# A banded attention step: the mask leaves the score product and becomes a multiplication of the exponentials on GpSimd

## The reference

```python
x = iter_norm_whiten(x, gamma, beta)             # whitening with a 64x64 matrix from the covariance
t = tokens(x)                                    # 16 x 3136 x 64
n = layernorm(t)                                 # queries, keys and values alike
windows = pad(n, 16)[:, arange(N)[:, None] + arange(33)[None, :]]
scores = einsum("bnd,bnwd->bnw", n, windows) * 64 ** -0.5
out = einsum("bnw,bnwd->bnd", softmax(scores), windows)
t = t + (layernorm(out) * gamma1 + beta1)
t = t + moe(layernorm(t))                        # 8 experts, the best 2 of each token, gelu
```

## Time and profile before

| what | value |
|---|---|
| median of the 3 runs | 1188.25 us (1186.55 to 1189.57) |
| the profiled execution: its own time, its span | 1198.36 us, 1196.5 us |
| mean granted clock of PE, of its full 2.4 GHz | 0.942 |
| PE busy | 1115.0 us, 93% |
| DVE busy | 913.3 us, 76% |
| ACT busy | 614.6 us, 51% |
| POOL busy | 146.7 us, 12% |

### The profile page before, as it was taken

How to read it: one execution, slowest core, us unless ns; L and a number is a source line. 1 busy time by engine, 2 the same in 40 slices (tenths; PEclk the granted TensorE clock), 3 DMA queues, 4 the chain that set the end, 5 groups by cost and what they waited for, 6 DMA issues and landing times.

```text
span 1196.5 us, 29077 instructions
## 1 busy us (share of the span) xinstructions
PE 1115.0 (93%) x9550; PEld 748.8 (63%) x9550; DVE 913.3 (76%) x2575; ACT 614.6 (51%) x975; POOL 146.7 (12%) x173
## 2 busy tenths in 40 slices
PE   7958999989899898989869999999999999999998
PEld 6836777777777777777655455555555555555553
DVE  6943678877777787878768877777787777777775
ACT  0015566656556565656435555555555555555553
POOL 6021222222222222222210000000000000000000
PEclk9957999999989898989759999999999999999999
DMA  9501121211211111211111222222222222222222
GB/s 291 195 22 27 48 60 50 61 48 46 61 44 51 47 54 47 54 47 35 37 54 39 69 69 68 68 68 69 69 69 69 69 68 68 68 69 69 69 69 47
DMA packets 136171, 78.69 MB, mean 66 GB/s; under 512 B 112416, under 2 KB 134176, under 8 KB 135344
## 3 DMA queue, kind: packets, MB, share of 16 engines
q1 hardware_dynamic: 127040, 64.78, 20.9%
q10 hardware_dynamic: 8064, 12.85, 2.9%
q0 software_dynamic: 1008, 0.43, 0.2%
HBM read 52.33 MB, written 25.69 MB: 65 GB/s over the span
## 4 chain that ended last, share of the span: by engine, by line
PE 64%; DVE 22%; ACT 5%; issue 5%; SPq 2%; DMA 1%; DVEq 0%; POOL 0%; ACTq 0%; POOLq 0%
PE p L1119 16%; PE p L1094 15%; PE p L1104 9%; DVE t_s L786 5%; PE p L1029 5%; PE p L1063 4%; PE p L934 3%; PE p L1041 3%; DVE sm L737 2%; PE p L927 2%; ACT prob L517 2%; DVE st L747 2%; PE p L1115 2%; DVE xn_s L780 2%; PE p L1058 2%
## 5 line engine op out<-in xcount | busy, mean ns | idle before, releaser
L546 ACT ACTIVATE arena<-p,b_s 128x896 f32<-128x896 f32 x224 | 225.4, 1007 | 245.9 <-PE p L1094 245.2
L843 DVE TENSOR_TENSOR arena<-arena,p 128x896 f32<-128x896 f32 x224 | 242.9, 1084 | 93.0 <-PE p L1104 89.8
L1119 PE MATMUL p<-arena,w_s 128*64 128x448 f32 x896 | 215.7, 560 | 0.3 <-DVE arena L843 0.3
L1094 PE MATMUL p<-thl,w_hi 128*128 128x448 f32 x448 | 165.0, 450 | 0.5 <-DVE thl L817 0.5
L1104 PE MATMUL p<-arena,selector 128*128 128x448 bf16 x448 | 124.7, 360 | 3.5 <-DVE arena L843 3.0
L1094 PE MATMUL p<-thl,w_lo 128*128 128x448 f32 x448 | 127.6, 366 | 0.0
L1104 PEld LDWEIGHTS p<-arena,selector 128*128 128x128 bf16 x448 | 25.5, 97 | 161.6 <-issue 116.1
L737 DVE TENSOR_REDUCE sm<-sq 128x14 f32<-128x896 f32 (+1 forms) x59 | 61.3, 1039 | 81.3 <-ACT sq L487 59.3
L1094 PEld LDWEIGHTS p<-thl,w_hi 128*128 128x128 f32 x448 | 85.8, 192 | 21.4 <-issue 1.0
L418 POOL TENSOR_TENSOR yb<-yb,bet 128x448 f32<-128x448 f32 x56 | 59.2, 1058 | 317.4 <-DVE xn_s L780 317.4
L1094 PEld LDWEIGHTS p<-thl,w_lo 128*128 128x128 f32 x448 | 84.9, 190 | 7.3
(11 more groups left out here) (174 smaller groups left out, 1817.5 us busy)
## 6 DMA issues: line engine op xcount, KB each, us to landing
tn_spill<-tnt_s ACTq DMA_DIRECT2D x56, 224.0 KB, 2.0
arena<-tn_spill SPq DMA_DIRECT2D x56, 224.0 KB, 3.4
t_s<-tn_spill SPq DMA_DIRECT2D x56, 224.0 KB, 2.5
arena<-in_x_dram SPq DMA_DIRECT2D x112, 96.0 KB, 2.1
out_dram<-arena SPq DMA_DIRECT2D x112, 96.0 KB, 1.8
resid<-in_x_dram SPq DMA_DIRECT2D x6, 1568.0 KB, 13.2
resid<-in_x_dram SPq DMA_DIRECT2D x6, 384.0 KB, 7.1
arena<-in_x_dram SPq DMA_DIRECT2D x112, 16.0 KB, 2.0
```

What stands on the lines that cost most here:

```text
L546: a.activation(hid[:, j % 2, :].rearrange("p (h n) -> p h n", h=H), (p34 if j % 2 == 0 else p56)[:, :, 0:CH], ACT.Gelu, bias=b1_s[:, j:j + ...
L843: v.tensor_tensor(gated[:, j % 2, :].rearrange("p (h n) -> p h n", h=H), hid[:, j % 2, :].rearrange("p (h n) -> p h n", h=H), p01[:, :, 0: ...
L1094: last = t.matmul(bank[:, h, 0:CH], w[:, 128 * j:128 * (j + 1)], thl[:, c, h, :], start=(k == 0), stop=(k == 1))
L1119: last = t.matmul(p2[64 * h:64 * h + 64, 0:CH], w2_s[:, j, :], gated[:, j % 2, h * CH:(h + 1) * CH], start=False, stop=(j == 3))
```

## The change

The mask product on PE goes, and with it the tile `outside`. Scores are no longer added to something; every one of their products starts its own sum. In its place POOL multiplies the exponentials, in place, by `band`, a 96x64 tile of ones and zeros that is laid over all 14 blocks of the chunk. This multiplication stands in POOL's step behind its two additions. PV waits for it (`s_pm`) and no longer for the exponentials.

```diff
@@ gpsimd, preparation @@
             v.tensor_copy(eye_h[:, :], eye[:, :])
-            v.tensor_scalar(outside[:, :].rearrange("p (n q) -> p n q", q=BLK),
-                            band[:, :].unsqueeze(1).to_broadcast([KEYS, 4 * H, BLK]), -1.0, OUTSIDE, ALU.add, ALU.mult)
@@ gpsimd, step(g, c, has) @@
                     v.tensor_tensor(resid[:, bass.ds(q * CH, CH)].rearrange("p (b c) -> p b c", b=NB), t_s[:, sl],
                                     yb[:, cq, :, 0:C], ALU.add).then_inc(s_t2, 1)
+                if has(2):
+                    q = g - 2
+                    wait(pool, s_p, q + 1)
+                    if has(3):
+                        wait(pool, s_t2, q)
+                    if has(1):
+                        wait(pool, s_yb, q + 2)
+                    scores = prob[:, :, :].rearrange("p h (b n) -> p (h b) n", b=NB)
+                    v.tensor_tensor(scores, scores, band[:, :].unsqueeze(1).to_broadcast([KEYS, H * NB, BLK]),
+                                    ALU.mult).then_inc(s_pm, 1)
@@ tensor, step(g, c, has) @@
                 if has(3):
                     q = g - 3
-                    wait(pe, s_p, q + 1)
+                    wait(pe, s_pm, q + 1)
                     wait(pe, s_vs, q + 1)
                     wait(pe, s_t, q)
...
                     wait(pe, s_kts, q + 2 if has(1) else q + 1)
                     wait(pe, s_p, q)
-                    for h in range(H):
-                        t.matmul(p34[0:KEYS, h, 0:CH], eye_h[0:KEYS, 0:KEYS], outside[:, 0:CH], start=True, stop=False)
                     for b in range(NB):
...
                             last = t.matmul(p34[0:KEYS, h, b * BLK:(b + 1) * BLK], keys_t[r, at_b:at_b + KEYS],
-                                            keys_t[r, at_b + WIN:at_b + WIN + BLK], start=False, stop=b == NB - 1)
+                                            keys_t[r, at_b + WIN:at_b + WIN + BLK], start=True, stop=True)
```

More of the change, by code:

```diff
@@ L49 @@
 ROUTE_GEXP = 3
-OUTSIDE = 16384.0
 def hybrid_kernel(nc, x, g0, b0, g1, b1v, rw, w1, b1, w2, b2, k_eye, k_fold, k_group, k_block, k_band,
@@ L93, in hybrid_kernel @@
         selector = sb("selector", [128, H * 4 * 128], bf16)
-        outside = sb("outside", [KEYS, 4 * H * BLK], bf16)
         eye_h = sb("eye_h", [128, 128], bf16)
@@ L218, in hybrid_kernel @@
         s_vt, s_vs, s_s, s_p, s_o = sem("v"), sem("v_copied"), sem("scores"), sem("probs"), sem("pv")
+        s_pm = sem("probs_masked")
         s_sqy, s_sq, s_t = sem("y_squared"), sem("pv_squared"), sem("t_scaled")
```

## The result

The changed kernel takes 1480.76 us (median of 4 runs, 1475.81 to 1484.34) against 1188.91 us before: a ratio of 1.244, 95% interval 1.238 to 1.251. The prediction was 1518 us, with a range of 1430 to 1580.

The account below looks back on a forecast made before the run. The attention round, a closed chain from PV through exponentials and t_s back to PV, was taken to bound; 55 rounds of 15.1 us against 502.4 give +328, plus 2 for the first PV: 1518 us, range 1430 to 1580.

Parts of the forecast that it names:

- The direction and the mechanism: Attention stage: PV would wait for POOL's multiplication behind L426; t_s to PV 5.8 us instead of 1.57; slower, chance 0.96.
- the sum: Attention round: 9.5 us from PV to t_s plus 5.8 back to PV, 15.3, taken as 15.1; 55 rounds, +328 us.
- The multiplication: POOL's new instruction on 896 columns: bounds 1.97 and 2.12 us, taken as 1.95 in the round.
- PE's stretch: PV to exponentials without the mask product: 3.92 us at full clock, 6.98 at half; most steps forecast at half.
- the tail: From the start of t_s to the next PV, through L426 and the multiplication: 5.8 us a round.
- low end: Scores at full clock in every round: 14.2 us a round, 1469 us; some rounds wholly at full clock bring it to 1430.
- The signs: Profile after: PV released by multiplication of 1.9 to 2.1 us, 4.4 us idle, exponentials 15 us apart, clock 0.5 to 0.7.
- That the clock matters: PE pauses before each PV put most steps at half clock; 2.6 us in each of 55 rounds hang on it.
- The clock rival: PE's clock stays up despite the pauses: rounds of 12.7 us, +196 us, 1386 us in all; chance 0.08.
- DVE's floor of 6.9 us at full clock: DVE's own work between PV and t_s keeps that stretch at 6.9 us at full clock, even without the mask product.
- The faster rival: Multiplication hidden between exponentials and next PV, only PE's gain left: 1153 us at most to win; chance 0.03.

Follow-up runs that it names:

- run 1: Changed kernel with POOL's multiplication moved to the front of its step, ahead of both additions: 1299.33 us, ratio 1.094 to the kernel before.
- run 5: Changed kernel with POOL multiplying only one block of fourteen (64 columns instead of 896), same place and waits: 1375.17 us, ratio 1.158 to the kernel before.
- run 7: Changed kernel with 72 small unused products ahead of PV, keeping PE busy through the pause: 1429.61 us, ratio 1.203 to the kernel before.
- run 3: Changed kernel without POOL's multiplication, so no mask at all, PV waiting for the exponentials: 1175.95 us, ratio 0.990 to the kernel before.
- run 12: Kernel before, its mask product kept on PE but issued earlier in the step, ahead of y: 1175.83 us, ratio 0.992.
- run 6: Changed kernel with 36 small unused products ahead of PV on PE: 1470.74 us, ratio 1.239 to the kernel before.

## Why the prediction was right, point by point

**The direction and the mechanism.** That the edge from t_s to PV would become t_s, routing operation and second norm, L426, multiplication, PV: shown. PV's releaser is the multiplication in all 56 steps, moving it to the front gives back 181 us net of the hold-up that it meets there (run 1), the duration at the old place enters one for one (run 5), and t_s to PV is 5.93 us on the mean against 5.8 in the sum. Its parts: 2.6 to L423 as taken, 1.17 to 1.20 from there to the multiplication against 1.16, 2.12 to PV against 2.05.

**The multiplication.** 2.066 us, between the bounds of 1.97 and 2.12, and a little over the 1.95 taken. The term was 0.1 us a round too small, 6 us in all.

**PE's stretch.** I took 3.92 us at full and 6.98 at half clock, and forecast most steps at half clock from PV to the scores. Measured are 5.4 to 5.8 us in most rounds and 6.98 in nine or so: the bound at half clock was exact, the share of it too high. In the timeline above the clock is back before the scores; PV and values alone are slow. With 2.50 us to t_s this is 8.31 us on the mean instead of the 9.3 in the sum. This is the mis-sized term: 1 us a round, some 55 us, partly offset by the 0.13 us by which the tail was longer. The range had this case as its low end (14.2 us a round). Part of the closeness of the total is luck: on the scale of the profiled executions the miss is 52 us (1528 forecast, 1476 measured), and only because the one before was 10 us above its median and the one after 5 us below is it 37 us on the scale of the medians.

**The signs.** The releaser, the length of the multiplication and the order on POOL came as listed. The exponentials are 14.2 us apart and not 15, PV's idle time is 215.2 us in 56 steps, 3.8 each and not 4.4, and the clock of the stage, 0.75, is above the 0.5 to 0.7 that I gave. PV to exponentials at 5.8 us is not near 7 us, which was one of my own signs of being wrong; it is the term above.

**That the clock matters.** Run 7 shows it: 51 us with its own losses included, and 1.87 us less in the stretch. The clock rival (1386 us) is out, since the clock does fall (0.75 in the stage).

**DVE's floor of 6.9 us at full clock** held, without effect on the sum. In run 3 the rounds at full clock take 6.95 us from PV to t_s in the median, as they do before, with the mask product gone. The exceptions are rounds without a routing operation, the first ones and one in seven after them, at 6.5 to 6.6 us.

**The faster rival** had a bound that holds (1153 us as the most to win; 1176 measured with no mask), but its condition was wrong. I wrote that it would decide "if the multiplication came before the additions". It came before them in run 1, ended ahead of PV, and the kernel was still 110 us slower than before, through DVE's held-up operations: exponentials to t_s grew from 2.75 to 4.46 us on the mean, nearly all of the 1.86 us by which the round grew. I had looked for the multiplication's users and not for DVE's instructions beside it. In the changed kernel itself the point has no effect: DVE has nothing to do while POOL multiplies.

## What to carry to other kernels

When work moves to an idle engine, look at what stands before it in that engine's list and when that is released, not at the engine's busy share; a 0.3 us instruction behind the wrong addition cost 3.2 us a round here. When a stretch is on the chain, first try to move work along its own engine's list into a wait that is already there (run 12), before moving it to another engine. And check which of DVE's instructions will run beside a long GpSimd one.

## What the runs showed of the hardware that I had not expected

A GpSimd instruction in progress holds up a VectorE instruction that reads two inputs in SBUF, until it ends: 1.80 us instead of 0.18 for 21 columns beside a multiplication of 2.08 us, 1.96 instead of 0.20 for 49 columns, 0.86 beside a copy of 0.87 us that has but one input. The price is that of the GpSimd instruction's length, not of the VectorE one's size; with seven short instructions the three small operations took 0.38 to 0.44 us each instead of 0.18. Not stretched were t_s, which has a PSUM input (1.43 us), and operations with a single SBUF input: beside POOL's second addition in run 1 the sum of 896 columns takes 1.09 us, as without it.

The Trainium skill's page "GPSIMD Engine Reference", section "1. Specifications", names contention with VectorE instructions that have two SBUF inputs; the traces agree, with the durations above. Had I held that line against the DVE instructions that would run beside the multiplication, I would have doubted the faster rival's condition.

PE's clock behind pauses, in rows: in run 6 PE stood idle for 2.25 us before PV; PV then took 1.04 us, but the values 1.46 and the scores 2.00, at a granted clock of 0.86 from 505 to 510 us and 0.79 from 510 to 515. In the changed kernel the pause was 4.36 us; PV and values behind it took 1.60 and 1.73 us, and the scores, 4.05 us after the restart, the 1.41 of full clock (0.89 from 505 to 510 us, 0.77 from 510 to 515). In the kernel before, half clock had lasted for some ten us around a pause of 2.4 us: it is 0.50 already from 393 to 394 us, while PE had been idle since 392.2. I had taken that one long stretch for the rule, and there the mis-sized term came from.
